# Self-attention of a two-block transformer: products and sums grouped in 11 blocks a step, 11 key tiles in GpSimd's partial sum

## The reference, cut to what matters

```python
scores = jnp.einsum('bqhd,bkhd->bhqk', qh, kh) / jnp.sqrt(jnp.asarray(d, q.dtype))
attn = jax.nn.softmax(scores, axis=-1)
out = jnp.einsum('bhqk,bkhd->bqhd', attn, vh)
```

## Time and profile before

| | us |
|---|---|
| median of three runs | 4157.27 |
| the profiled execution, device time | 4159.49 |
| its span, first to last instruction | 4157.7 |
| TensorE busy | 3771.6 |
| VectorE busy | 2333.9 |
| ScalarE busy | 1867.3 |
| GpSimd busy | 2080.2 |
| maxima L1957, 2048 of them | 1275.0 |
| adds L2029, 256 + 32 | 1172.1 + 146.8 |
| products L1832, 4096 matmuls | 547.2 |

### The profile page before, as it was taken

One profiled execution on the slowest core, in us unless ns is written; L12 is line 12 of the kernel. 1 busy time (PEld: TensorE's weight loads), 2 busy tenths in 40 slices (PEclk: granted clock), 3 DMA queues, 4 the chain that ended last, 5 costly groups with the idle time before them and its releaser, 6 DMA issues. The chain is left out here.

```text
span 4157.7 us, 58861 instructions
## 1 busy us (share of the span) xinstructions
PE 3771.6 (91%) x19596; PEld 2442.6 (59%) x19596; DVE 2333.9 (56%) x4020; ACT 1867.3 (45%) x3431; POOL 2080.2 (50%) x923
## 2 busy tenths in 40 slices
PE   4799969979999999999999999985999959999998
PEld 2577748854444444444444444433777737888887
DVE  2466642247777767776777777733676625222222
ACT  1465631115666656665666666663565521111111
POOL 0356630005778767776777777783676634000000
PEclk8788879978999999999999999997999869999999
DMA  7566657752130211203130211105567651211110
GB/s 230 133 158 173 168 154 220 227 137 62 26 67 16 64 27 38 46 23 67 26 67 15 65 26 26 31 18 134 135 165 173 164 166 56 81 40 40 40 40 30
DMA packets 213560, 371.98 MB, mean 89 GB/s; under 512 B 36103, under 2 KB 52999, under 8 KB 209703
## 3 DMA queue, kind: packets, MB, share of 16 engines
q1 hardware_dynamic: 213287, 368.49, 32.7%
HBM read 215.54 MB, written 144.51 MB: 87 GB/s over the span
## 5 line engine op out<-in xcount | busy, mean ns | idle before, releaser
L1957 DVE TENSOR_REDUCE a_peak<-a_sm 128x1 f32<-128x512 f32 x2048 | 1275.0, 682 | 470.5 <-PE a_sm L1797 464.5
L1911 ACT ACTIVATE a_e<-a_st 128x512 f32<-128x512 f32 x2048 | 1075.1, 600 | 718.2 <-PE a_st L1819 714.7
L2029 POOL TENSOR_TENSOR a_esum<-a_esum,a_e 128x2048 f32<-128x2048 f32 x256 | 1172.1, 4578 | 126.5 <-ACT a_e L1911 114.1
L1819 PE MATMUL a_st<-a_q,a_k 128*128 128x512 f32 x2048 | 870.2, 428 | 17.9 <-issue 12.9
L1797 PE MATMUL a_sm<-a_k,a_q 96*128 96x512 f32 x2048 | 831.8, 413 | 49.7 <-DMA a_k<-s_k 28.1
L1819 PEld LDWEIGHTS a_st<-a_q,a_k 128*128 128x128 f32 x2048 | 386.4, 189 | 536.7 <-ACT a_e L1911 269.9
L1832 PE MATMUL a_acc<-a_e,a_v 128*32 128x512 f32 x4096 | 547.2, 606 | 17.6 <-ACT a_sums L1925 16.7
L1797 PEld LDWEIGHTS a_sm<-a_k,a_q 96*128 96x128 f32 x2048 | 397.8, 194 | 148.8 <-DVE a_peak L1957 57.6
L2152 PE MATMUL mlp_ph<-mlp_us,mlp_w_hi 128*128 128x512 f32 x1024 | 336.3, 391 | 31.9 <-DVE mlp_raw_lo L2201 31.9
L2029 POOL TENSOR_TENSOR a_esum<-a_e 128x2048 f32<-128x2048 f32 x32 | 146.8, 4587 | 427.6 <-ACT a_e L1911 427.6
L2194 ACT ACTIVATE mlp_gelu<-mlp_ph,mlp_b 128x512 f32<-128x512 f32 x128 | 88.1, 688 | 595.4 <-PE mlp_ph L2152 595.4
(11 more groups left out here) (151 smaller groups left out, 5169.7 us busy)
## 6 DMA issues: line engine op xcount, KB each, us to landing
p_qs<-s_q SPq DMA_DIRECT2D x192, 256.0 KB, 5.7
s_q<-p_qo SPq DMA_DIRECT2D x64, 512.0 KB, 7.4
a_q<-s_q SPq DMA_DIRECT2D x96, 256.0 KB, 5.2
a_k<-s_k SPq DMA_DIRECT2D x24, 1024.0 KB, 15.5
s_x<-p_x SPq DMA_DIRECT2D x16, 1024.0 KB, 4.4
s_u<-p_ut_hi SPq DMA_DIRECT2D x64, 256.0 KB, 5.8
s_u<-p_ut_lo SPq DMA_DIRECT2D x64, 256.0 KB, 6.4
p_us<-s_u SPq DMA_DIRECT2D x16, 1024.0 KB, 7.8
```

The costliest lines, as they stand in the source:

```text
L1819: pe.matmul(st[0:KR, place(kt, h) % RING], k[:, g % 2, h, kt * P:kt * P + KR], q[:, j % QR, h], start=True, stop=True).then_inc(score_done, 1)
L1911: act.activation(e[0:KR, (j * NKT + kt) % ER, h], st[0:KR, place(kt, h) % RING], ACT.Exp, scale=SCALE).then_inc(score_read, 1)
L1957: dve.tensor_reduce(dst, src, AX.X, ALU.max).then_inc(unit_read, 1)
L2029: pool.tensor_tensor(esum[:], e[:, slot(0)] if x == 1 else esum[:], e[:, slot(x)], ALU.add).then_inc(e_added, 1)
```

## The change

Four things change, all in `attention`.

- POOLED, the tiles whose exponentials GpSimd adds, becomes 0, 1, 2, 4, 5, 7, 8, 10, 11, 12, 13 (eleven tiles, ten adds); it was 0, 1, 3, 4, 6, 7, 9, 10, 12, 13 (ten tiles, nine adds). TensorE sums tiles 3, 6, 9, 14 and 15 and the partial sum; it was 2, 5, 8, 11, 14, 15 and the partial sum. GpSimd's scaling stands after seven adds; it was after five.
- The block after head 1 of each key tile is replaced by a list, `products`. Blocks stand at key tiles 0, 1, 2, 4, 5, 7, 8, 10, 11, 13 and 15, with two pieces each (a piece being eight matmuls of `weigh`, of `add_up` or of `add_partial`). At key tiles 3, 6, 9, 12 and 14 there is none. The last sums and the last product of a step are issued at tiles 0 and 1 of the next step, and product 0 at tile 2.
- DIVIDE_AT goes from (6, 8, 32) to (10, 12, 36), in units.
- ScalarE's `fetch_sums` moves from after tile 0 to after tile 1 of the next step.

```diff
--- before.py
+++ after.py
@@ -1614,7 +1614,7 @@
     QR = 4
     ER = 4
 
-    POOLED = [t for t in range(NKT - 2) if t % 3 != 2] if NKT > 2 else []
+    POOLED = [0, 1, 2, 4, 5, 7, 8, 10, 11, 12, 13]
     ADDS = max(len(POOLED) - 1, 0)
     STEPS = B * GROUPS * CHUNKS
     BODY = 2 * CHUNKS
@@ -1624,7 +1624,7 @@
     TILES = GH * NKT + 1
     RING = 3
     LATE = 1 if NKT > 1 else 2
-    DIVIDE_AT = (6, 8, 32) if NKT > 1 else range(4)
+    DIVIDE_AT = (10, 12, 36)
     SETUP = 2 + KW % 2
     with nc.cleanup_on_exit(), ExitStack() as ctx:
         sb = lambda n, s, t=F32: ctx.enter_context(nc.sbuf_tensor(f"{name}_{n}", s, t))
@@ -1836,25 +1836,60 @@
 
             def add_up(i, j, kt):
 
-                if kt in POOLED:
-                    return
                 first = min(t for t in range(NKT) if t not in POOLED)
-                operands = [e[0:KR, (j * NKT + kt) % ER]]
-                if POOLED and kt == NKT - 1:
-                    pe.wait_ge(e_added, (BODY * i + j + 1) * ADDS)
-                    operands.append(esum)
-                for x, operand in enumerate(operands):
-                    for h in range(GH):
-                        mm = pe.matmul(acc[h * DH:(h + 1) * DH, 1], ones[0:KR], operand[:, h], start=(kt == first),
-                                       stop=(kt == NKT - 1 and x == len(operands) - 1), tile_position=(0, h * DH))
+                for h in range(GH):
+                    mm = pe.matmul(acc[h * DH:(h + 1) * DH, 1], ones[0:KR], e[0:KR, (j * NKT + kt) % ER, h], start=(kt == first),
+                                   stop=False, tile_position=(0, h * DH))
+                if kt < NKT - 1:
+                    mm.then_inc(tile_used, 1)
+
+            def add_partial(i, j):
+
+                pe.wait_ge(e_added, (BODY * i + j + 1) * ADDS)
+                for h in range(GH):
+                    mm = pe.matmul(acc[h * DH:(h + 1) * DH, 1], ones[0:KR], esum[:, h], start=False, stop=True, tile_position=(0, h * DH))
                 mm.then_inc(tile_used, 1)
+
+            def products(i, j, kt):
+
+                if kt == 0 and exists(i, j - 1):
+                    add_up(i, j - 1, 14)
+                    weigh(i, j - 1, 15)
+                elif kt == 1 and exists(i, j - 1):
+                    add_up(i, j - 1, 15)
+                    add_partial(i, j - 1)
+                elif kt == 2 and exists(i, j):
+                    weigh(i, j, 0)
+                    weigh(i, j, 1)
+                elif kt == 4 and exists(i, j):
+                    weigh(i, j, 2)
+                    weigh(i, j, 3)
+                elif kt == 5 and exists(i, j):
+                    add_up(i, j, 3)
+                    weigh(i, j, 4)
+                elif kt == 7 and exists(i, j):
+                    weigh(i, j, 5)
+                    weigh(i, j, 6)
+                elif kt == 8 and exists(i, j):
+                    add_up(i, j, 6)
+                    weigh(i, j, 7)
+                elif kt == 10 and exists(i, j):
+                    weigh(i, j, 8)
+                    weigh(i, j, 9)
+                elif kt == 11 and exists(i, j):
+                    add_up(i, j, 9)
+                    weigh(i, j, 10)
+                elif kt == 13 and exists(i, j):
+                    weigh(i, j, 11)
+                    weigh(i, j, 12)
+                elif kt == 15 and exists(i, j):
+                    weigh(i, j, 13)
+                    weigh(i, j, 14)
 
             def step(i, j):
                 turn = exists(i, j + 1)
                 units = units_of_step(i, j)
                 given, scores = 0, 0
-                if NKT == 1 and exists(i, j - 1):
-                    weigh_tiles(i, j - 1, [0])
                 for kt in range(NKT):
                     for h in range(GH):
                         if exists(i, j):
@@ -1863,21 +1898,12 @@
                         while given < len(units) and given * GH * NKT < scores * U:
                             score_unit(i, *units[given])
                             given += 1
-                        if NKT > 1 and h == 1:
-                            if kt == 0 and exists(i, j - 1):
-                                weigh_tiles(i, j - 1, [NKT - 1])
-                            if kt > 0 and exists(i, j):
-                                weigh_tiles(i, j, [kt - 1])
+                        if h == 1:
+                            products(i, j, kt)
                     if kt == TURN_KT and turn:
                         turn_peaks(i, j + 1)
                 for m, u in units[given:]:
                     score_unit(i, m, u)
-
-            def weigh_tiles(i, j, tiles):
-
-                for kt in tiles:
-                    weigh(i, j, kt)
-                    add_up(i, j, kt)
 
             pe.sem_inc(tile_used, ER)
             pe.wait_ge(small_in, 2 * DMA)
@@ -1925,14 +1951,12 @@
                 act.activation(sums[:, j % 2], acc[:], ACT.Copy).then_inc(acc_read, 1)
 
             def step(i, j):
-                if NKT == 1 and exists(i, j - 1):
-                    fetch_sums(i, j - 1)
                 for kt in range(NKT):
                     if exists(i, j):
                         exponentials(i, j, kt)
-                    if NKT > 1 and kt == 4 and exists(i, j - 1):
+                    if kt == 4 and exists(i, j - 1):
                         spread_inverse(i, j - 1)
-                    if NKT > 1 and kt == 0 and exists(i, j - 1):
+                    if kt == 1 and exists(i, j - 1):
                         fetch_sums(i, j - 1)
                     if kt == TURN_KT and exists(i, j + 1):
                         take_rows(i, j + 1)
@@ -2036,12 +2060,12 @@
 
             def step(i, j):
                 if POOLED and exists(i, j):
-                    for x in range(1, 6):
+                    for x in range(1, 8):
                         add(i, j, x)
                 if exists(i, j - LATE):
                     scale(i, j - LATE)
                 if POOLED and exists(i, j):
-                    for x in range(6, len(POOLED)):
+                    for x in range(8, len(POOLED)):
                         add(i, j, x)
 
             pool.sem_inc(scaled, 2)
```

## The result

The changed kernel takes 4379.95 us, median of four runs (4366.61 to 4387.18), against 4157.52 for the kernel before (4156.93 to 4166.01, four runs). The ratio is 1.0526, 95% interval 1.0498 to 1.0555: it is 5.3% slower. The profiled execution is the fastest of the four, 4366.61, with a span of 4364.8. That is 207 over the span before. The last scaling comes 218 later than before (3024.98 for 2806.62) and what follows it takes 11 less, though nothing was changed there.

What follows compares the result with a forecast made beforehand. TensorE was taken as the busy engine that bounds the kernel. Step: 56.4 + 5.8 (hold) + 2.7 (clock) = 64.9 us, +7.5; 4159.5 + 228 - 2.2 = 4385 us, range 4165 to 4530.

Steps and rivals of the forecast that it cites:

- The hold: VectorE's peak chain after unit 49: negation passes at 7.6, then GpSimd's add of tile 11 holds the copy until 12.2.
- The rule behind it: Two-port copies and two-SBUF-input VectorE instructions can't run beside GpSimd reading SBUF; whoever starts first keeps the port throughout.
- Unit 8 of the stretch: TensorE's last peak unit between the blocks at tiles 11 and 13: due at 7.6, starts at 13.4, 5.8 us late.
- Clock: TensorE's idle stretch of over 5 us in each step lowers its clock to 1.2 GHz: 2.7 us, bounds 0 and 2.7.
- Late units: Stretches of eight pairs from tiles 2, 5 and 8 wait for VectorE's maxima: 1.0, 0.3 and 1.0, together 2.3 us.
- The saving of the blocks: TensorE, 11 blocks of two pieces instead of 16 blocks with 23 pieces: 2.4 us a step removed.
- The end: Last step, where nothing covers GpSimd's adds: ten closed adds end at 47.7 against 44.8, so +3 us once.
- Sum: Step 64.9 us, +7.5; 30 x 7.5 + 3 = 228 us more in all, giving 4385 us.
- 1: Two GpSimd adds hold the peak chain: step 69.5 us, +12.1 x 30 + 3, 4523 us; chance 0.22.
- 2: One add holds the chain but the clock stays: step 62.2 us, +4.8 x 30 + 3, 4304 us; chance 0.14.
- Rival 3: Nothing is held on VectorE, the stretches eat the saving: step 57.7 us, +0.3 x 30 + 3, 4169 us; chance 0.13.
- 4: Faster: VectorE's queue hides in the blocks, peaks cost 0.9 as now: step 55.0 us, 4088 us; chance 0.13.

Runs made afterwards that it cites:

- peaks_unit50: Changed kernel with HEAD 13 for 14, so the peaks end with unit 50 instead of 49 and the negation is due 0.6 us later; 4386.66 us, ratio 1.0555.
- peaks_unit47: Changed kernel with HEAD 16 for 14, so the peaks end with unit 47 and the negation is due 1.2 us earlier; 4259.11 us, ratio 1.0239.
- block_first: Changed kernel, but at key tile 13 the block of two products is issued before unit 53 instead of behind it; 4281.89 us, ratio 1.0305.
- even_blocks: As negate_on_gpsimd, with the same 11 blocks evenly spaced, one after every sixth score, and the division's parts moved; 4078.97 us, ratio 0.9808.
- negate_before: Kernel before, only the negation, copy and low part of the peaks made by GpSimd after its add of tile 10; 4127.53 us, ratio 0.9927.
- negate_on_gpsimd: Changed kernel with the negation, copy and low part of the peaks made by GpSimd after its scaling, not VectorE; 4151.55 us, ratio 0.9984.

## Why the prediction was right, point by point

- *The hold.* Right in place, instruction and number. The negation was forecast 7.5 after the first score behind the block at tile 10, the add of tile 11 at 7.6; they came 7.47 and 7.55 after 1836.12. The negation passed by 0.08 us. That it did was luck, and behind the loop it did not: there the negation was held 4.56. The forecast said that the copy would then be held by a second add, 16.9 after zero. This step of it was wrong where it could be seen: the copy followed the negation after 0.03 and passed at the same border. The loop's distance of 0.13 is too long for that, as peaks_unit50 shows, so the price hung on the 0.08.
- *The rule behind it.* The Trainium skill (SBUF — State Buffer, "Who interferes with whom") names copies in a two-port mode among what can't run beside GpSimd. The trace agrees so far as the copy was held (L1996 at 4.33); in which mode it ran, no trace here shows.
- *Unit 8 of the stretch.* Forecast 5.8 late, measured 5.45, mainly since the maxima went on 12.3 after zero and not 12.6.
- *Clock.* Forecast 2.7, read from a loop's turn; measured 2.8 in the same step. peaks_unit47 shows that it is a cost of its own, and with block_first that it is paid after shorter waits too: some 1.6 after a wait of 1.8 in every second step.
- *Late units.* Forecast 1.0, 0.3 and 1.0, together 2.3. In the changed kernel's own step the stretches from tiles 2, 5 and 8 took 6.89, 6.19 and 6.80, where eight pairs and a block of two pieces make 5.83: 1.06, 0.36 and 0.97, together 2.4. The first of them, in starts of scores on TensorE:

```profile
1808.38 0.50 PE L1819 MATMUL a_st<-a_q,a_k 128*128 128x512 f32 x1
...
1815.27 0.51 PE L1819 MATMUL a_st<-a_q,a_k 128*128 128x512 f32 x1
```

- *The saving of the blocks.* 2.4 a step on TensorE was right as a sum of pieces: a stretch of four pairs and two pieces takes 3.93 in the changed kernel, as before. As a gain it never showed whole: even_blocks at 54.9 is 1.5 below negate_before at 56.4.
- *The end.* +3 for the last adds was not found: the last two distances between scalings are 55.7 and 20.9, together 76.6, against 79.0 before.
- *Sum.* 30 x 7.5 + 3 = 228 forecast; 222 measured between the medians, and 207 between the two profiled executions. The steps with the loop's turns take 71.1 and 70.7, only 4.6 over before. At the first turn itself TensorE waited 6.44 before and now 1.71 and 0.70; why it waits less there stays open.
- *Rivals.* 1 fell by the negation that passed, 2 by the granted clock of 0.50, 3 and 4 by L1996. Rival 3's kernel without a hold exists, negate_on_gpsimd, at 4152 for its 4169.

## What to carry to other kernels

Before filling a GpSimd gap, ask which short VectorE instructions run in it: once GpSimd is closed, a dependent chain of such small instructions paid one whole GpSimd instruction, or two where the next link missed the border between two adds. Give such a chain to the engine that would hold it, or put it where that engine waits for data.

When products are gathered in fewer blocks, the length of the stretch between them is what the slowest partner's ring has to bear. Here six pairs all but fit three banks (0.1 late) and eight did not (0.4 to 1.1 late), so the same 11 blocks were worth nothing in gaps of four and eight and 2.5 us a step in gaps of six. What stopped TensorE for 5 us also cost it the clock for the next six, so that wait was worth about half as much again as it measured.

## What the runs showed of the hardware that was not expected

- A VectorE instruction may start while a GpSimd instruction is in its last tenth of a microsecond: the negation ran from 1843.59 to 1843.76 over the scaling's end at 1843.71. Started 0.08 or more before the next add it passed in 24 steps of the changed kernel; started 0.03 or less before it, it was held to the add's end in the last six. Started 0.02 after the scaling's start, in peaks_unit47, it took 1.29.
- The distance from the negation's end to the copy's start was 0.13 to 0.14 in the loop and 0.03 to 0.04 outside it. With the longer one the copy missed the border between two adds, with the shorter one it passed. It decided between one hold and two (61.2 and 66 a step in peaks_unit50).
- The clock stayed whole through 3.2 us of idle TensorE in block_first and fell as work resumed; the slow time was 3.5 there and six in the changed kernel. In peaks_unit47 waits of 1.80 and 1.82 in neighbouring steps had different ends: the clock fell behind the first and not behind the second.
